# First score pass of an attention and mixture-of-experts block: contraction over 64 rows, two heads in the two row halves of the array

## What is computed

```python
q, k, v = split(x @ W_in.T + b_in)            # 16 heads, 64 wide each
q, k = rope(q), rope(k)                       # rotary tables
att = softmax(where(causal, q @ k.T / 8, -inf))
x = layernorm(x + (att @ v) @ W_out.T + b_out)
x = layernorm(x + experts(x))                 # gate: top 3 of 16, width 256 -> 512 -> 256
```

## Time and profile before

| | before |
|---|---|
| median of 3 runs | 1840.57 us (1835.0 to 1841.21) |
| the profiled execution, first to last instruction | 1831.6 us |
| TensorE busy (matmul) | 1689.9 us, 92% |
| VectorE busy | 1381.3 us, 75% |
| GpSimd busy | 1233.2 us, 67% |
| ScalarE busy | 728.9 us, 40% |
| mean granted TensorE clock | 0.958 |

### The profile page before, as it was taken

The page is one execution under the profiler, slowest core; times in us unless marked ns, Lnnn a source line. Parts: engine busy times, 40 slices in busy tenths (PEclk is TensorE's granted clock), DMA queues, the critical chain, the costliest instruction groups (busy, mean ns, idle before and its releaser), DMA issues. The chain is left out here.

```text
span 1831.6 us, 34098 instructions
## 1 busy us (share of the span) xinstructions
PE 1689.9 (92%) x9515; PEld 1265.2 (69%) x9516; DVE 1381.3 (75%) x3236; ACT 728.9 (40%) x1551; POOL 1233.2 (67%) x1064
## 2 busy tenths in 40 slices
PE   4699999999999999999999999998659999999990
PEld 4566667666766677666766676664249999999980
DVE  3578888888888888988888898885775566556654
ACT  2244444444444544444444444543352222222222
POOL 2266787677877776788777777764017777777764
PEclk8699999999999999999999999999759999999995
DMA  9975566655755776556776564531954444444448
GB/s 310 336 217 151 162 170 201 171 173 157 190 150 177 229 219 190 157 164 199 211 218 187 173 185 139 162 104 50 369 158 72 73 74 72 71 73 74 71 65 278
DMA packets 185571, 302.37 MB, mean 165 GB/s; under 512 B 23632, under 2 KB 82896, under 8 KB 185312
## 3 DMA queue, kind: packets, MB, share of 16 engines
q1 hardware_dynamic: 161872, 269.20, 49.5%
q0 software_dynamic: 21504, 30.29, 10.4%
q10 hardware_dynamic: 2064, 1.31, 0.3%
HBM read 188.81 MB, written 111.67 MB: 164 GB/s over the span
## 5 line engine op out<-in xcount | busy, mean ns | idle before, releaser
L798 ACT ACTIVATE prob<-b_ps 128x512 f32<-128x512 f32 (+3 forms) x768 | 354.4, 488 | 357.0 <-PE b_ps L607 255.8
L534 POOL TENSOR_TENSOR acc<-acc,prob 128x1024 f32<-128x1024 f32 (+1 forms) x192 | 353.0, 1839 | 6.4 <-POOL acc L534 3.7
L606 PE MATMUL b_ps<-q,k 128*128 128x512 f32 (+3 forms) x768 | 295.8, 389 | 4.8 <-ACT prob L798 3.5
L507 POOL TENSOR_TENSOR roped<-rot 128x512 f32<-128x512 f32 x128 | 174.7, 1365 | 164.1 <-DVE rot L937 163.1
L599 PE MATMUL a_ps<-k,q 128*128 128x512 f32 (+3 forms) x768 | 266.2, 383 | 16.9 <-DMA k<-scratch_hilo 6.7
L688 PE MATMUL y_ps<-prob,v_sb 128*64 128x512 f32 (+3 forms) x1536 | 272.9, 490 | 0.1
L917 DVE CUSTOM_DVE_ANT_0 masked<-a_ps,causal 128x128 bf16<-128x128 f32 (+3 forms) x512 | 237.2, 478 | 42.7 <-PE a_ps L599 35.2
L607 PE MATMUL b_ps<-q,k 65*128 65x512 f32 (+3 forms) x768 | 264.2, 348 | 0.0
L1487 POOL DMA_INDIRECT scratch_sum<-y,dst_i x112 | 186.5, 1665 | 96.2 <-ACT y L1559 90.4
L966 DVE RECIPROCAL inv<-inv 128x128 f32<-128x128 f32 x256 | 232.2, 929 | 7.7 <-ACT inv L839 5.3
L512 POOL TENSOR_TENSOR lo<-roped,hi 128x512 fp32r<-128x512 f32 x128 | 177.0, 1383 | 81.2 <-ACT hi L811 81.2
(11 more groups left out here) (258 smaller groups left out, 2393.6 us busy)
## 6 DMA issues: line engine op xcount, KB each, us to landing
q<-scratch_hilo SPq DMA_DIRECT2D x192, 256.0 KB, 4.6
k<-scratch_hilo SPq DMA_DIRECT2D x192, 256.0 KB, 5.2
scratch_hilo<-hi SPq DMA_DIRECT2D x64, 512.0 KB, 4.0
scratch_hilo<-lo SPq DMA_DIRECT2D x64, 512.0 KB, 4.7
w_sb<-scratch_wsplit SPq DMA_DIRECT2D x32, 512.0 KB, 3.7
w<-in_L_ffn_W_dram SPq DMA_DIRECT2D x32, 512.0 KB, 10.1
wv_sb<-scratch_wsplit SPq DMA_DIRECT2D x16, 512.0 KB, 6.2
xT<-scratch_xsplit SPq DMA_DIRECT2D x6, 1024.0 KB, 6.6
```

Source lines behind the costliest of these rows:

```text
L534: nc.gpsimd.tensor_tensor(sums, old, probs(q), ALU.add).then_inc(m["sum_p"], 1)
L606: nc.tensor.matmul(out, k1[s][:, h, js], q1[s][:, h, qs], start=True, stop=False, skip_group_check=True)
L798: nc.scalar.activation(probs(q)[:, h, :], b_ps[:, h, 0:w], ACT.Exp).then_inc(exp_done[h], 1)
```

## The change

The first score pass contracts over 64 rows, high parts only. Head 0's product lies in array rows 0 to 63, head 1's in rows 64 to 127, and both are issued one behind the other, at the place in TensorE's list where head 1's product stood; the entry of head 0 is skipped. VectorE's list is unchanged. For head 1, `k1` now holds k_lo above and k_hi below; this takes six transfers in `stack` in place of four, of the same bytes in all. The second pass sums the same products as before.

```diff
@@ stack
-                    for dst, src in ((q1[s][0:64], q_hi), (q1[s][64:P], q_hi), (k1[s][0:64], k_hi), (k1[s][64:P], k_lo)):
+                    for dst, src in ((q1[s][0:64], q_hi), (q1[s][64:P], q_hi), (k1[s][0:64, 0], k_hi[:, 0]),
+                                     (k1[s][64:P, 0], k_lo[:, 0]), (k1[s][0:64, 1], k_lo[:, 1]), (k1[s][64:P, 1], k_hi[:, 1])):
                         sp.dma_start(part(dst, c).bitcast(F32), src).then_inc(qk_ld[c][s], 16)
@@ query_scores
-                nc.tensor.matmul(out, q1[s][:, h, blk * P:(blk + 1) * P], k1[s][:, h, k0:k0 + w], start=True,
+                rows = slice(64 * h, 64 * h + 64)
+                nc.tensor.matmul(out, q1[s][rows, h, blk * P:(blk + 1) * P], k1[s][rows, h, k0:k0 + w], start=True,
                                  stop=True, skip_group_check=True).then_inc(a_fill[h], 1)
@@ the tensor engine's turn
                         h = int(e[-1])
+                        if h == 0:
+                            continue
                         if q in (0, 4):
-                            pe.wait_ge(qk_ld[q // 4][s], 64 * (n // 2 + 1))
-
-                        wait_for(pe, a_max[h], UNITS * n + q, n if q else n - 1)
-                        query_scores(s, h, q)
+                            pe.wait_ge(qk_ld[q // 4][s], 96 * (n // 2 + 1))
+                        for h in range(2):
+                            wait_for(pe, a_max[h], UNITS * n + q, n if q else n - 1)
+                        for h in range(2):
+                            query_scores(s, h, q)
```

More of the change, by code:

```diff
@@ L332, in put_halves @@
                 if n >= 2:
-                    sp.wait_ge(qk_ld[c][s], 64 * (n // 2))
+                    sp.wait_ge(qk_ld[c][s], 96 * (n // 2))
                     sp.wait_ge(qk2_ld[c][s], 32 * (n // 2))
```

## The result

The changed kernel takes **2307.6 us** (2303.4 to 2314.1, 4 runs) against 1838.9 us (4 runs): ratio 1.256, 95% interval 1.254 to 1.259. It is 469 us slower; the forecast was 336 us, and the time lies above the range. The direction and the kind of cause were right, the size was not.

The account below looks back on a forecast made before the run. TensorE, busy 100 of 100 us, was taken to bound the kernel. Exchanges of 282 us plus 54 us of low clock made 336 on 1840.6: 2176, stated as 2175 us, with an 8-in-10 range of 2065 to 2260.

Parts of the forecast that it names:

- Direction and main cause: Score pairs: slower (chance 0.95), since both products wait for both heads' maxima while VectorE's list keeps head 0's maximum early.
- The four other exchanges that VectorE sets: Waits between neighbouring units: 9 to 10 2.5 us, 10 to 11 2.5, 11 to 0 1.9, 0 to 1 1.4.
- the exchange sum of 9.2 us: All intervals between units together: 9.2 us a step added, 46.1 in place of 36.95; 282 us with the ends.
- the four intervals that I left to TensorE: Units 1 to 2, 2 to 3, 6 to 7, 8 to 9: stay TensorE's, change by -0.35 us in all.
- The step that failed: the clock: TensorE around unit 5: clock falls in most steps, costing 1.8 us a step, 54 us; bounds 0 and 4 us.
- 6 us for both ends: The two steps at the ends of the run: 6 us added together, beside 30 full steps of 9.2 us.
- O1 waits for G1: Unit 5 to 6: O1 waits for G1, which stands behind M5.0 and r2 on VectorE, done at 2.6 us.
- my chain over r3 and M5.1: Unit 5 to 6: M5.0, r2, r3, M5.1, o1, then X0 sets the interval, 6.3 us in place of 2.17.
- The transfers: `stack`'s six in place of four: costed at nothing; without cover up to 2.6 us a step.
- rival 4: Score pairs: the two row halves don't run together, 21 to 45 us on top, about 2210 us; chance 0.10.
- rival 2: Score pairs: doubled array pays, VectorE's slack swallows the rest; 2.1 us a step given back, 1774 us; chance 0.04.
- Rival 3: Exchanges: waits partly absorbed, 4 to 6.5 us a step, 1961 to 2036 us; chance 0.10.

Follow-up runs that it names:

- Order alone: Changed kernel's order of issue, both heads' products at head 1's place, but each product over all 128 rows, no row halves: 2197.9 us, ratio 1.197.
- VectorE's list alone: Changed kernel with VectorE's list put in TensorE's order, each unit's two maxima together behind work not needing them: 1915.2 us, ratio 1.043.
- the run with the well filled gaps: Changed kernel with TensorE's gaps filled by unread products behind unit 4's pair, O1 and unit 9's maximum, and ahead of units 11, 0, 1: 2190.8 us, ratio 1.193.
- the best with paired heads: Changed kernel with VectorE's list in TensorE's order and products over all 128 rows, one behind the other: 1866.2 us, ratio 1.017.
- moving one word of VectorE's list: Changed kernel with head 0's maximum of unit 5 moved behind r3 in place of ahead of r2: 2117.7 us, ratio 1.154.
- the run with unit 3 repaired: Changed kernel with head 0's maximum of unit 3 moved behind k1, k2 and r0 in place of ahead of them: 2255.6 us, ratio 1.229.

## Why the prediction was right or wrong

**Direction and main cause: right, shown.** Order alone gives 362 us; VectorE's list alone takes 392 back. The interval between units, reckoned and as the run with the well filled gaps shows it at full clock:

| interval | reckoned | at full clock | changed kernel |
|---|---|---|---|
| unit 3 to F1 | 7.4 | 7.62 | 7.61 |
| F1 to unit 5 | 7.56 | 7.62 | 9.21 |
| unit 5 to 6 | 6.3 | 6.32 | 7.12 |
| unit 6 to 7 | 5.76 as before, or up to 0.35 less | 5.81 | 7.82 |
| unit 7 to 8 | 4.2 | 4.21 | 3.75 |

The four other exchanges that VectorE sets came within 0.3 us in the changed kernel itself (9 to 10: 2.8 for 2.5; 10 to 11: 2.6 for 2.5; 11 to 0: 2.0 for 1.9; 0 to 1: 1.3 for 1.4). At full clock a step is 47.5 us against 46.1 reckoned; the exchange sum of 9.2 us was 1.4 short. Half of it, 0.7 us, lies in the four intervals that I left to TensorE (units 1 to 3, 6 to 7, 8 to 9: 13.0 us, reckoned 12.3), where the way out of a pair costs 0.19 us in place of 0.1; 0.35 lies at unit 9 to 10, 0.22 at unit 3 to F1, the rest is tenths. Some 0.2 us of the 1.4 is the filling itself.

**The step that failed: the clock.** "I expect that the clock falls there in most steps and that 3 to 4 us of the work behind ... run at 1.2 GHz; half of this is lost: 1.8 us a step." It fell at a second place too, behind the thin stretch ahead of F1, and stayed low 6.8 us behind unit 5: 10.2 us in all, and 12.0 on average, since some steps have more. Reading the last two columns of the table at F1 to unit 5, 5 to 6 and 6 to 7, it costs 1.6 + 0.8 + 2.0 = 4.4 us; 0.5 comes back at 7 to 8, so 3.7 to 4 us net (51.2 - 47.5). Filling the gaps measured it at 117 us, not 54. My bounds for it, 0 and 4 us, held that price; the range did not, since it took the upper end of one term without the others'. At least 63 us of the miss of 133 are the clock's. The expectation that the clock falls was right; its place was half right, and its size was the error.

**The rest of the miss,** some 70 us: 30 steps times 1.4 us, 42, are the exchanges' and the layout's. The first step accounts for most of what remains: from the first product of the second pass to the same one a step later it is 58.1 us in place of 35.1, where I had put 6 us for both ends. 27 us of it run at 1.2 GHz, also in the run with the gaps well filled (59.6 us), so the clock has a part in this that the 117 us do not contain; how large it is stays open.

**One reading was wrong, and luck hid it.** I wrote that O1 waits for G1. It waits for G0 (in the listing `2 * n + q // 2 + 1`, and q is 1): O1 follows the pair at once, at 394.69. TensorE's long wait stands one further, at B6.1, for the exponential behind h2, which hangs on the same r2. I had not reckoned this chain at all. At full clock it brings TensorE to X0 at 524.72 (0.23 us behind the last product of B), and o1, the end of my chain over r3 and M5.1, at 524.78: X0 starts at 524.84, so my chain sets the 6.32 us, but by 0.1 us only. In the changed kernel the other one sets the interval: o1 is done at 400.45, and TensorE, slow behind B6.1, comes to X0 at 401.20.

**The transfers** at nothing: right (ratio 0.999). **Side by side:** rival 4 is excluded. **Doubled array pays** (rival 2): excluded even with the waits repaired. The Trainium skill, TensorEngine Tiling (Array Packing), Theoretical Speedup, gives up to 2x for a contraction of at most 64; here the two products do run together, and the pass still loses. The Trainium skill, TensorEngine Tiling (Array Packing), Key Properties, says that a change of mode drains the engine; the rows agree in that each change costs time. Measured, it is 0.29 us a visit against at most 0.23 us gained. **What the profile would show:** steps of 46 to 48 us: 51.2. VectorE's waits on `a_ps` 12 us a step: 19. TensorE waiting 2 us at O1: none, it is the 3.51 us at B6.1. 1.5 us at B4.1: 1.56. L599's (now L601's) busy time half: no, 266 to 185 us, and 174 where the clock stays up; the mean record of a product grew from 383 to 473 ns (444 there).

Rival 3 (partly absorbed) has no support: at full clock every interval of the table came out as long as reckoned or longer. **What stays open:** what decides that the clock falls. In the step shown it fell behind a stretch whose longest gaps were 0.45 and 1.56 us; the runs show where, not the rule. Why the low clock grew when the wait at unit 3 was repaired is open with it. No version here beats the kernel before; the best with paired heads is 1866 us.

## What to carry to other kernels

When one engine's hand-written order moves, lay the other engine's list beside it: an instruction whose input now comes later blocks finished work behind it, and moving one word of VectorE's list was worth 190 us here (another only 52). Count a visit to a row half with its way in and out (0.1 + 0.19 us) before counting what side by side saves (0.23 us at 512 columns); here lone pairs between full products lost. And where TensorE comes to wait often, put a price on the clock too: here it cost 117 us beside some 355 of waits and layout, and it swallowed half of what the repair of one wait should have given back.

## What the runs showed of the hardware

- Products of 64 rows in different row halves start 3 ns apart and run together; in the same half, 512 columns, they start 0.34 us apart. Two full products alone as a pair start 0.30 us apart, in a stream 0.23.
- Going from products over 128 rows to one of 64 rows costs 0.10 us (seen at 128 columns), the way back 0.19 us at 128 and some 0.20 at 512 columns.
- A step can settle on a length. In the changed kernel and in the run with unit 3 repaired, 15 and 19 of 31 steps last 51.2 us to a tenth, with 10 and 17 us of low clock: less waiting was met by more low clock. In the kernel with the gaps well filled most steps are 47.5 us.
